# A four-tile transpose block issued in two halves on neighbouring steps, in a graph-attention kernel on one core

## What is computed

```python
A_tilde = A + jnp.eye(n, dtype=A.dtype)
mask = A_tilde > 0
Wh = (H @ W.T).reshape(n, HEADS, D_K)
score_l = jnp.einsum('nhd,hd->nh', Wh, a_l)
score_r = jnp.einsum('nhd,hd->nh', Wh, a_r)
e = score_l[:, :, None] + score_r.T[None, :, :]
e = jnp.where(e >= 0, e, NEG_SLOPE * e)
e = jnp.where(mask[:, None, :], e, -jnp.inf)
alpha = jax.nn.softmax(e, axis=2)
out = jnp.einsum('nhm,mhd->nhd', alpha, Wh).reshape(n, OUT_DIM)
...
x = _layernorm(x + _L0_gnn_ref(x, adj, L0_gnn_W, L0_gnn_a_l, L0_gnn_a_r), axis=-1)
```

## Time and profile before

| | |
|---|---|
| time of three runs | 1781.74, 1785.81 and 1786.43 us, median 1785.81 |
| the profiled execution | 1786.13 us |
| its span, first to last instruction | 1784.3 us |
| PE / PEld busy | 1649.9 us (92%) / 1626.8 us (91%) |
| DVE busy | 1685.1 us (94%) |
| ACT busy | 1667.3 us (93%) |
| DMA issues of SP | 256 of 1 MB for blocks, 448 for `vring` |

### The profile page before, as it was taken

One profiled execution on the slowest core, in us unless ns is written; L12 is line 12 of the kernel. 1 busy time (PEld: TensorE's weight loads), 2 busy tenths in 40 slices (PEclk: granted clock), 3 DMA queues, 4 the chain that ended last, 5 costly groups with the idle time before them and its releaser, 6 DMA issues. The chain is left out here.

```text
span 1784.3 us, 80971 instructions
## 1 busy us (share of the span) xinstructions
PE 1649.9 (92%) x37067; PEld 1626.8 (91%) x37067; DVE 1685.1 (94%) x1905; ACT 1667.3 (93%) x1246; POOL 26.2 (1%) x36
## 2 busy tenths in 40 slices
PE   6887988899998999999999999999999999999995
PEld 6787888898998999999999999999999998999995
DVE  6999999997989989899999989999999999999997
ACT  4999999899899999999999999999999999999992
POOL 0000000000001000000000100000000100000000
PEclk9999999999999999999999999999999999999998
DMA  9995887999998786675766676666667122121111
GB/s 285 339 351 183 294 283 265 337 307 328 302 319 294 249 253 203 197 240 185 244 194 229 201 240 201 221 205 217 229 194 241 40 82 58 37 58 37 34 37 37
DMA packets 241476, 368.10 MB, mean 206 GB/s; under 512 B 12912, under 2 KB 103408, under 8 KB 239600
## 3 DMA queue, kind: packets, MB, share of 16 engines
q1 hardware_dynamic: 241136, 362.92, 62.6%
HBM read 345.57 MB, written 17.30 MB: 203 GB/s over the span
## 5 line engine op out<-in xcount | busy, mean ns | idle before, releaser
L505 ACT ACTIVATE bmask<-lrow,rtab 128x2048 fp8e4<-128x2048 f32 (+1 forms) x975 | 1548.0, 1667 | 39.4 <-PE psum L414 37.4
L414 PE MATMUL psum<-vring,cmask 128*128 128x99 bf16 x14336 | 718.0, 208 | 39.7 <-DVE cmask L730 28.5
L414 PE MATMUL psum<-vring,bmask 128*128 128x99 bf16 x14336 | 719.4, 207 | 10.8 <-DMA vring<-v_scratch 6.8
L414 PEld LDWEIGHTS psum<-vring,cmask 128*128 128x128 fp8e4 x14336 | 660.9, 98 | 52.1 <-DVE cmask L730 38.3
L414 PEld LDWEIGHTS psum<-vring,bmask 128*128 128x128 fp8e4 x14336 | 667.1, 97 | 13.8 <-DMA vring<-v_scratch 7.7
L730 DVE SCALAR_TENSOR_TENSOR cmask<-acache,bmask 128x1024 int32<-128x1024 int32 x512 | 633.1, 1237 | 25.1 <-PE psum L414 25.0
L725 DVE SCALAR_TENSOR_TENSOR bmask<-acache,bmask 128x1024 int32<-128x1024 int32 x512 | 633.8, 1238 | 6.7 <-ACT bmask L505 3.0
L706 DVE TENSOR_SCALAR bmask<-lrow,rtab 128x2048 fp8e4<-128x2048 f32 (+1 forms) x305 | 321.8, 1071 | 0.0
L383 PE MATMUL trp<-pack,abuf 128*128 128x64 bf16 x4096 | 145.6, 194 | 27.4 <-issue 14.5
L383 PEld LDWEIGHTS trp<-pack,abuf 128*128 128x128 bf16 x4096 | 133.9, 99 | 30.2 <-issue 28.6
L414 PE MATMUL psum<-vt,cmask 128*128 128x99 bf16 x2048 | 106.5, 210 | 15.1 <-DVE cmask L730 7.5
(11 more groups left out here) (64 smaller groups left out, 264.5 us busy)
## 6 DMA issues: line engine op xcount, KB each, us to landing
abuf<-in_adj_dram SPq DMA_DIRECT2D x256, 1024.0 KB, 8.2
vring<-v_scratch SPq DMA_DIRECT2D x384, 99.0 KB, 3.2
lrow<-l_scratch SPq DMA_DIRECT2D x16, 1024.0 KB, 8.2
v_scratch<-vt SPq DMA_DIRECT2D x16, 792.0 KB, 11.2
vring<-v_scratch SPq DMA_DIRECT2D x64, 198.0 KB, 7.1
cmask<-in_x_dram SPq DMA_DIRECT2D x16, 256.0 KB, 5.1
late<-in_x_dram SPq DMA_DIRECT2D x16, 256.0 KB, 5.2
out_dram<-late SPq DMA_DIRECT2D x16, 256.0 KB, 3.6
```

The costliest lines, as they stand in the source:

```text
L414: return nc.tensor.matmul(psum[:, bank, at * S3:(at + 1) * S3], mask[:, j * P:(j + 1) * P], values, start=opening, stop=True, skip_group_c ...
L505: last = nc.scalar.activation(to, rows, ACT.Relu, bias=rtab[:, 2 * s + i, H + h:H + h + 1], scale=BIG, saturate=False)
```

## The change

For blocks 0 to 15 nothing changes. A block from 16 on is turned in two pieces of two column tiles. The first piece (16 matmuls, with the waits for the block and for the empty `trp`) stands where the whole turn stood, between the b and the c group of its step. The second piece (16 matmuls, no wait of its own) stands at the head of the next step, ahead of that step's waits and its b group. `tr_done` is raised by the last matmul of the second piece. No instruction is added or taken away but for the split, and no list of SP, DVE or ACT changes.

```diff
-            def turn_block(n):
-
-                pe.wait_ge(a_loaded[n % 2], 32 * (n // 2 + 1))
-                wait(pe, evac_done, n)
-                for k in range(BITS):
+            def turn_block(n, bits=range(BITS)):
+
+                if bits[0] == 0:
+                    pe.wait_ge(a_loaded[n % 2], 32 * (n // 2 + 1))
+                    wait(pe, evac_done, n)
+                for k in bits:
                     for j in range(SUB):
...
-                last.then_inc(tr_done, 1)
+                if bits[-1] == BITS - 1:
+                    last.then_inc(tr_done, 1)
...
+                for n in TURNED[q - 1] if q > 0 else []:
+                    if n >= QUADS:
+                        turn_block(n, range(BITS // 2, BITS))
                 if w < JUST_MADE:
                     pe.wait_ge(v_lo, q // EVERY_STEPS + 1)
...
                 for n in TURNED[q]:
-                    turn_block(n)
+                    turn_block(n, range(BITS) if n < QUADS else range(BITS // 2))
```

## The result

The changed kernel takes 1839.2 us, the median of 4 runs (1836.45 to 1842.22). The kernel before took 1786.12 us in the same comparison (4 runs, 1781.74 to 1788.84). The ratio is 1.0295 (95% interval 1.0276 to 1.0314), so the change costs 53 us, 3%. The profiled execution of the changed kernel has 1842.22 us and a span of 1840.4 us, 56 us more than that of before.

What follows compares the result with a forecast made beforehand. The prediction took PE to bound the largest stretch the change can act on, 600 to 1400 us (busy 781 of 800). Its terms, 1786.1 + 0 + 55 + 12 - 1, gave 1852 us, with a range of 1818 to 1882.

Steps and rivals of the forecast that it cites:

- 55 forecast: Stretch 600 to 1400 us (steps 146 to 394): PE's new waiting for values that land later, 55 us.
- 12 forecast: Stretch 305 to 600 us (steps 64 to 146): missing parts of the values' margin add up to 12 us.
- a rival: Stretch 600 to 1400 us: each of 62 new waits lowers the clock, 105 us on top, 1957 us; chance 0.02.

## What to carry to other kernels

A semaphore that one engine raises may hold a whole list of another: when its producer is moved, read on in that list past the waiting entry, here to a 99 KB load that stood behind 2 MB and was needed in four steps. Before the last matmul of a group is moved by t, take for every later use the margin between landing and use; the new waiting is about the sum of (t - margin) where it is positive, however small the waits in the profile are (6.8 us stood there in all). It becomes time where the engine that waits has hardly a pause to give up (55 forecast, 48.3 measured), and perhaps not where it has many (12 forecast, 11.6 of waiting, and as much less in pauses). And if a small urgent load shares a queue with a large patient one, put it first or give it one slot more: either took back all 53 us.

## What was not expected

The waits did reach the clock, but in a few places and not in all 62, as a rival had it. One place in the kernel before, behind the wait of 2.56 us, became four in the changed kernel, from the wait ahead of step 64 to step 394. Of the 54 waits between 605 and 1450, a stretch with a mean granted clock of 1.00, one was followed by a lower clock, that of 1.92 us. The timeline of the changed kernel has it, with the two longer ones ahead of that stretch of which the first stands above:

```profile
340.30 2.85 PE L416 MATMUL psum<-vring,bmask 128*128 128x99 bf16 x32 [3.58 <-DMA vring<-v_scratch]
...
1346.41 2.41 PE L416 MATMUL psum<-vring,bmask 128*128 128x99 bf16 x32 [1.92 <-DMA vring<-v_scratch]
```

The busy time by window (columns as above), next to the window of 0.61 that stands above, and behind the wait of 1.92 us:

```profile
314.00:320.00 6.00, 6.00 (x150) 6.00 (x147) 6.00 (x9) 5.61 (x7) 0.00 (x0) 1.00 0.79 234
...
1345.00:1351.00 6.00, 4.59 (x74) 4.59 (x74) 6.00 (x6) 4.00 (x3) 0.00 (x0) 0.72 0.10 24
```

At 0.61 the clock is mostly at the lower of its two levels, 1.2 GHz, and 6 us further it is back at 2.4: 85 matmuls in the first 6 us and 150 in the next. Such a place costs some 2 us (6 x 0.39 = 2.3, 6 x 0.28 = 1.7). At 340.30 and 1346.41 the group of 32 matmuls takes 2.85 and 2.41 us where others take 1.60.

The second surprise is the ring: a fifth slot gives 4 to 5 us (0.9976 and 0.9977) to a kernel whose profile shows only 6.8 us of waits for that load, while issuing the same loads first gives it nothing. By the times of the steps both gain in steps 146 to 394 (792.6 and 794.8 us against 799.6); in steps 64 to 146, where a block comes every 2.4 steps, the fifth slot takes 295.8 us and the loads first 301.9, against 295.0. These are single traces: they say where to look and not why.
